# Twenty-five background steps of the next batch move from the experts' tile loop into the first feed-forward

## What is computed

```python
# block 0
h = layernorm(x) * (1 + ca) + sa
x = x + ga * attn_topk(h)        # 16 heads of 16; of each row of scores only the 32 largest count
h = layernorm(x) * (1 + cb) + sb
probs = softmax(h @ Wg + bg); e = argmax(probs) % 8
x = x + gb * relu(h @ We[e] + be[e]) * max(probs)      # "first feed-forward", 8 experts
# block 1
h = layernorm(x) * (1 + ca) + sa
x = x + ga * attn_wide(h)        # 16 heads of 64, softmax over all causal scores
h = layernorm(x) * (1 + cb) + sb
h = h + attn_small(layernorm(h) * w)                   # 16 heads of 16
y = h + moe(layernorm(h) * w2)   # router, the best 2 of 8 experts, gelu, hidden width 512
x = x + gb * y
```

## Time and profile before

| | us |
|---|---|
| three timed executions | 5928.27, 5930.14, 5935.34 |
| their median | 5930.14 |
| the profiled execution, as timed | 5932.03 |
| the profiled execution, span of its instructions | 5930.3 |

### The profile page before, as it was taken

One profiled execution on the slowest core, in us unless ns is written; L12 is line 12 of the kernel. 1 busy time (PEld: TensorE's weight loads), 2 busy tenths in 40 slices (PEclk: granted clock), 3 DMA queues, 4 the chain that ended last, 5 costly groups with the idle time before them and its releaser, 6 DMA issues. The chain is left out here.

```text
span 5930.3 us, 83316 instructions
## 1 busy us (share of the span) xinstructions
PE 4491.5 (76%) x30341; PEld 2890.1 (49%) x30341; DVE 4104.7 (69%) x8455; ACT 2753.8 (46%) x6035; POOL 1908.1 (32%) x1563
## 2 busy tenths in 40 slices
PE   4444478988677678988777688998777686999776
PEld 2333345666434454666533454666533453666334
DVE  6999957887787656888688656887778655222630
ACT  2444424666244533666345351666445360554333
POOL 2565512444323421444323430444333431000001
PEclk7656689999788889999888788999888797999888
DMA  3000000000301120000121121000031201000312
GB/s 124 11 12 25 1 22 25 18 13 15 57 12 63 48 96 22 15 16 18 36 33 35 69 76 48 13 13 13 15 54 32 75 30 50 16 10 10 63 63 72
DMA packets 113333, 213.59 MB, mean 36 GB/s; under 512 B 25728, under 2 KB 70632, under 8 KB 109552
## 3 DMA queue, kind: packets, MB, share of 16 engines
q1 hardware_dynamic: 104736, 190.94, 11.8%
q0 software_dynamic: 6144, 16.79, 0.9%
q10 hardware_dynamic: 2048, 0.53, 0.0%
HBM read 154.38 MB, written 49.73 MB: 34 GB/s over the span
## 5 line engine op out<-in xcount | busy, mean ns | idle before, releaser
L1492 DVE MAX8 vals<-work 128x8 f32<-128x128 f32 (+7 forms) x1536 | 1080.7, 743 | 0.4
L1866 POOL TENSOR_SCALAR keep<-ssb,vals 128x128 bf16<-128x128 f32 (+7 forms) x512 | 876.4, 1723 | 0.0
L469 PE MATMUL ring<-ident,pr 128*128 128x128 f32 x2304 | 490.9, 334 | 423.8 <-POOL pr L1871 372.2
L1506 DVE MATCH_REPLACE8 work<-vals,work 128x128 f32<-128x128 f32 (+7 forms) x1024 | 750.6, 739 | 0.0
L1853 POOL TENSOR_TENSOR pool_step<-ones 128x2 f32<-128x2 f32 x256 | 50.0, 195 | 2132.1 <-DVE vals L1492 2131.6
L576 PE MATMUL pA<-SC 128*128 128x512 f32 (+3 forms) x1536 | 615.6, 510 | 82.8 <-DVE SC L1635 42.3
L1871 POOL TENSOR_TENSOR pr<-keep,pr 128x128 f32<-128x128 bf16 (+7 forms) x512 | 649.0, 1289 | 0.0
L469 PEld LDWEIGHTS ring<-ident,pr 128*128 128x128 f32 x2304 | 334.8, 171 | 573.4 <-POOL pr L1871 395.5
L1143 ACT ACTIVATE prT<-ring 128x512 f32<-128x512 f32 (+1 forms) x768 | 380.5, 498 | 407.2 <-PE ring L469 405.8
L1621 DVE TENSOR_REDUCE nmax<-pA 128x1 f32<-128x1024 f32 (+7 forms) x512 | 384.4, 751 | 259.6 <-PE pA L577 248.0
L1492 DVE MAX8 vals<-ssb 128x8 f32<-128x128 f32 (+7 forms) x512 | 363.0, 750 | 263.7 <-ACT ssb L1131 246.8
(11 more groups left out here) (225 smaller groups left out, 7968.9 us busy)
## 6 DMA issues: line engine op xcount, KB each, us to landing
SC<-in_w SPq DMA_DIRECT2D x64, 512.0 KB, 7.3
stage<-parts SPq DMA_DIRECT2D x384, 64.0 KB, 2.4
parts<-SC SPq DMA_DIRECT2D x72, 256.0 KB, 2.5
SC<-parts SPq DMA_DIRECT2D x144, 128.0 KB, 7.9
SC<-in_wqkv SPq DMA_DIRECT2D x32, 384.0 KB, 2.9
rows_out<-SC SPq DMA_DIRECT2D x92, 128.0 KB, 1.7
SC<-rows_in SPq DMA_DIRECT2D x20, 512.0 KB, 3.9
SC<-in_ffn_we SPq DMA_DIRECT2D x4, 2048.0 KB, 10.3
```

The source lines that it names most:

```text
L469: mm = pe.transpose(r[:, blk % 4 * P:blk % 4 * P + P], pr0[:, p % 2, blk * P:blk * P + P], ident[:, :])
L1492: m = v.max(vals0[:, y, i, 8 * n:8 * n + 8], src[:, lo:hi])
L1506: done[i] = cht.mark(v.match_replace(out=work0[:, lo:hi], in_to_replace=vals0[:, y, i, 8 * n:8 * n + 8], in_values=src[:, lo:hi], imm_valu ...
L1866: pool.tensor_scalar(keep0[:, lo:hi], ssb0[:, p % 2, lo:hi], vals0[:, p % 2, i, TOPK - 1:TOPK], None, ALU.is_ge).then_inc(s["k"], 1)
```

## The change

The background gets a new place, called "ffn", with 8 points and a share of 0.05 of the 493 ticks, ahead of all others. The share of the experts' loop falls from 0.19 to 0.14. The other shares keep their size, so each stage between the two carries the same number of ticks as before, but from a tick 24.65 further on. Each engine gets calls `at("ffn", t)` in the first feed-forward: PE after the bias product of tile t, DVE after the update of X of tile t, ACT and SP in a row after their own work there, and POOL between the two halves of the norm that follows, which is cut in two for it. The due ticks at the eight points are 3, 6, 9, 12, 15, 18, 22, 25.

```diff
--- before.py
+++ after.py
@@ -138,8 +138,8 @@
 class Pace:
 
 
-    STAGES = (("wide", 8 * 17, 0.51), ("prep", 12, 0.04), ("flip", 8 + 48, 0.22), ("route", 6, 0.04),
-              ("moe", 23, 0.19))
+    STAGES = (("ffn", 8, 0.05), ("wide", 8 * 17, 0.51), ("prep", 12, 0.04), ("flip", 8 + 48, 0.22), ("route", 6, 0.04),
+              ("moe", 23, 0.14))
 
     def __init__(self):
         self.at, done = {}, 0.0
@@ -524,7 +524,7 @@
                     if end:
                         at("prep", t)
 
-            def ffn(b):
+            def ffn(b, at):
                 emptied(("n1", b, 3))
                 for t in range(NT):
                     if t >= 2:
@@ -561,6 +561,7 @@
                         pe.wait_ge(f0["x"], b * NT + t)
                     pe.matmul(pV[:, 0:D], gT[:, t * P:t * P + P], be[:, :], start=True, stop=True)\
                       .then_inc(f0["yb"], 1)
+                    at("ffn", t)
 
             def wide(b, at):
                 s = a1
@@ -838,7 +839,7 @@
                 pe.wait_ge(t0["nm"], b * 8 + 8)
                 project(b, [oall0[:, g, :] for g in range(4)], 4, wo0, t0, False, at)
                 norm("n1", b)
-                ffn(b)
+                ffn(b, at)
                 norm("n2", b)
                 wide(b, at)
                 project(b, oall_w, 8, wo1, a1, True, at)
@@ -1041,6 +1042,8 @@
                 sp.dma_start(we, ffn_we).then_inc(f0["w"], 16)
                 if b + 1 < B:
                     narrow_parts(0, b + 1, lambda name, i: None)
+                for t in range(NT):
+                    at("ffn", t)
                 sp.wait_ge(f0["x"], b * NT + NT)
                 sp.dma_start(wo1, wo[1]).then_inc(a1["wo"], 16)
                 wide(b, at)
@@ -1839,12 +1845,14 @@
             c.mark(pool.memset(vall0[:, :, 0:16 * VC].rearrange("p t (h d) -> p t h d", d=VC)[:, :, :, 16], 1.0))
             assert c.n == N_CONST
 
+            def half_norm(n, b, h):
+                pool.wait_ge(ln[n]["var"], b * 2 + h + 1)
+                pool.tensor_tensor(rstd[:, 4 * h:4 * h + 4], ve[:, 4 * h:4 * h + 4], mhalf[:, 0:4], ALU.pow)\
+                    .then_inc(ln[n]["rs"], 1)
+
             def norm(n, b):
-
                 for h in range(2):
-                    pool.wait_ge(ln[n]["var"], b * 2 + h + 1)
-                    pool.tensor_tensor(rstd[:, 4 * h:4 * h + 4], ve[:, 4 * h:4 * h + 4], mhalf[:, 0:4], ALU.pow)\
-                        .then_inc(ln[n]["rs"], 1)
+                    half_norm(n, b, h)
 
             carried, chosen, normal = [0], [0], [0]
 
@@ -1956,7 +1964,10 @@
                 pool.wait_ge(pj[0]["dr"], min(b + 2, B) * 192)
                 pool.wait_ge(s_x, b * 16 + 16)
                 pool.memset(qm, 0.0).then_inc(s_qz, 1)
-                norm("n2", b)
+                for h in range(2):
+                    for t in range(4 * h, 4 * h + 4):
+                        at("ffn", t)
+                    half_norm("n2", b, h)
                 wide(b, at)
                 for t in range(NT):
                     at("prep", t)
```

## The result

The changed kernel takes 5956.1 us (median of 6 runs, 5955.1 to 5958.4) against 5930.6 us (5928.3 to 5938.5) of the kernel before on the same chip: a ratio of 1.0040, 95% interval 1.0029 to 1.0052. It is slower by 0.4%, where the forecast was 5922 us. The two profiled executions have spans of 5930.3 and 5955.5 us.

A forecast was written before the change was run, and what follows sets the result against it. No engine bounds the whole span; PE paces the first feed-forward, DVE is busiest in the small attention. Batch 0 +1.0, batches 1 and 2 -4.5 each, together -8.0 us: 5924.0 from 5932.0, 5922 against the median; range 5888 to 5952.

The forecast's parts named there:

- The first feed-forward: First feed-forward: 25.6 us of DVE ticks, 8.9 hidden in its idle, the rest lengthens the stage: +16.8 us a batch.
- POOL's cover: First feed-forward: POOL's two selections fit between the half norms at no cost; if not, up to 6 us a batch.
- The wide attention: Wide attention: same 251 ticks without the empty first ones, groups starting at other phases: 577.6 against 565.7, +11.9 us.
- its classes: Wide attention: group lengths fall in two classes by first tick's phase, mean 71.5 us at r = 3, 65.1 at r = 0.
- The rival of the classes: Wide attention: the two classes are not real; 58 us in all at full price, half gives 5951; chance 0.14.
- The preparation: Preparation: the second reciprocal and spread leave it for the wide attention's group 7; -5 us, upper end 7.0.
- The small attention: Small attention: keeps 109 full ticks and its spread; 0, with -5 to +5 us for the phase.
- The routing: Routing: selections come between the scatter DMAs, the last scatter starts 6.3 us later, the following wait shortens; +3 us, at most +6.3.
- The experts' loop: Experts' loop: fewer ticks and less PE idle, 125 us; -25.7 us in batch 0, -31.2 in batches 1 and 2.
- The lower clock's 5 us: Experts' loop, batches 1 and 2: 5 us of longer PE busy time at a lower clock, counted as gained.
- The rival of a longer selection loop: Experts' loop: a selection step spans one tile more, 4.15 us; 12 us a batch, 36 in all, 5958; chance 0.14.
- PE's clock in the feed-forward: First feed-forward rival: new waits halve PE's clock, 4 us in each of five tiles, 60 us in all, 5982; chance 0.05.

The follow-up runs named there:

- the 14-tick kernel: Changed kernel with later spreads, but 14 ticks in the first feed-forward, taken from the wide attention, experts' loop share as before: 5910.2 us, ratio 0.9961.
- the one spread out of POOL's way: Changed kernel with only the small attention's spread moved, from k = 378 to k = 381: 5939.0 us, ratio 1.0020 to the kernel before.
- later spreads: Changed kernel with the three inner spreads three ticks later, the last two later: 5920.9 us; the same three inner moves in the kernel before: 5922.3 us.
- the half norm ahead of the selection: The 14-tick kernel, but POOL gives the norm's second half before its last feed-forward point: 5900.4 us, ratio 0.9956 to the kernel before.
- 13 ticks: Later spreads, ticks 0 to 12 in the first feed-forward, taken from the wide attention; tick 13 with POOL's selection stays there: 5929.7 us, ratio 0.9999.

## Why the prediction was wrong, step by step

**The first feed-forward was right.** +17.1 to +18.3 measured, +16.8 forecast. DVE no longer waits for PE from tile 3 on and runs its ticks in full; a tile of three ticks takes 9.9 to 10.4 us on DVE. POOL's cover held there as written, since both selections lie clear of the half norms; the 14-tick kernel shows what it costs when it does not, 3.6 us a batch, within the 6 that the text named. Up to the last update of X the stage grew by 12.9 us for the 12.5 forecast.

**The wide attention was 2 to 4 us short**, and its classes were half right. The changed kernel's groups, first to last (three of eight rows):

```profile
944.70:1016.00 71.30, 63.29 (x461) 41.96 (x462) 51.62 (x101) 44.22 (x104) 24.34 (x20) 0.96 0.03 8
...
1155.90:1223.10 67.20, 61.29 (x492) 43.04 (x490) 55.68 (x105) 45.37 (x106) 27.24 (x23) 0.97 0.03 8
...
1365.70:1441.80 76.10, 65.20 (x503) 45.52 (x502) 59.65 (x116) 47.98 (x111) 32.55 (x28) 0.94 0.10 28
```

Group 0 is 71.3 where 71.5 was forecast, group 3 67.2 for 65.1, group 6 76.1 for 71.5, and group 4 with its spread 72.7 for 78.5. The classes of the earlier trace rows do not carry over to other phases to better than 6 us a group; the sum came out well since the errors went both ways (-5.8 in group 4, +4.6 in group 6), which is luck. The rival of the classes was the right doubt, at 8 us in all of the 58 of its full price.

**The preparation** won 8 to 9 us for 5, more than the 7.0 named as its bound. The spread and the reciprocal left it, as the text said; why they are worth more than 7.0 there was not tried.

**The small attention was the step that failed.** The text said "The small attention keeps 109 ticks and its spread, all of them full before and after: 0". The count was right and the conclusion wrong. The spread moved from the last slots of the stage into its third head group, and what one pays for it is set by what stands ahead of it on POOL (6.1 us of selection) and behind it on ACT (the stage's exponentials). The term was 0 and measured +6.8, +8.9 and +10.6 us. With the one spread out of POOL's way, 17 of the 25 us are gone and the stage is within 1 to 3 us of before; what the rest comes from stays open. The bound of 5 us a batch, taken for "the phase", came from no row. One was at hand: a selection and the scatter behind it lie 6.3 us apart, and a whole selection ahead of POOL's multiplication would have given that as the upper end for the spread in this stage; with the multiplication's 1.27 us, which the rows did not show, it is 7.6, near the 7.96 measured. I had priced that very chain in the wide attention, at 7.0 for a reciprocal and a spread, as if it were a fixed cost.

**The routing was right**: +2.5 to +3.6 for +3, by the selection that came between the scatters. From the first scatter to the last it is 31.4 us for 25.4, 6.0 more where 6.3 was forecast, and the loop starts 8.0 us after the last one, as forecast.

**The experts' loop was right in mechanism and a little too hopeful**: 127 to 129 us for 125, 2 to 4 over. PE is busy 119.4 us of 127.4 in batch 0, where 118.9 was the sum, and idle 8.0, where I took 6. The lower clock's 5 us of batch 1 and 2 were gained, as counted. The rival of a longer selection loop, the one on the slow side with a place of its own, did not happen.

**PE's clock in the feed-forward**: the mean fell from 0.91 to 0.85, and one tile's matmuls of batch 0 took 9.95 us instead of 7.13. The changed kernel's clock by stretches, from the windows view:

```profile
865.30:906.30 41.00, 37.85 (x96) 15.85 (x94) 34.11 (x83) 5.17 (x10) 3.93 (x4) 1.00 0.00 1
906.30:913.10 6.80, 5.70 (x7) 2.52 (x8) 6.52 (x17) 0.43 (x1) 3.17 (x3) 0.50 0.00 1
913.10:930.20 17.10, 14.50 (x44) 6.27 (x42) 16.59 (x39) 3.93 (x8) 4.96 (x5) 1.00 0.00 0
930.20:944.70 14.50, 3.94 (x16) 3.14 (x16) 13.00 (x34) 3.12 (x5) 2.15 (x2) 0.50 0.19 72
```

So the clock was at its lower level for 6.8 us, from within a wait of PE of 2.62 us (one tile before, it had waited 1.60), and again for the last 14.5 us, in which PE waits 10.9 us for the norm; before, that last stretch is 7.6 us long, with a wait of 4.4. The rival had one such tile right where it feared five. The Trainium skill, "TensorE: Matmul & The Clock Gate", section "HAM oscillation — how this bites in real kernels", describes a loop in which a wait brings TensorE back to its low clock in every turn. This trace agrees only in part: PE waited in two of the last five tiles and not in all, for less time than in the page's loop, and one tile ran slow. It cost nothing that the trace shows: DVE had no idle for line 546 from tile 3 on, since its tile takes longer still. The tile in PE's timeline of the changed kernel:

```profile
907.40 9.95 PE L546 MATMUL pA<-SC,hT 128*128 128x512 f32 x16 [2.62 <-DVE SC L1597]
917.28 0.69 PE L562 MATMUL pV<-be,SC 8*128 8x256 f32 x2
```

## What to carry to other kernels

When background work is shifted along a schedule, list not only how much of it each stage carries, but each rare event in it with a wait of its own, and for each, before and after, what stands ahead of it on the engine it waits for and what stands behind the waiting instruction. A short step that others wait for belongs ahead of a long one on an in-order engine, or a few ticks behind it: here moving four such steps was worth 35 us in the changed kernel and 8 us in the kernel before, where they happened to lie better. Moving 25 ticks made no difference that could be told once they were out of the way. Count the idle that is there before filling it, and then look at what the moved ticks do elsewhere: with the same later spreads and from the same place, the experts' loop, 14 ticks gave a kernel 0.28% faster than before and 25 gave 0.1%. The fastest, at 0.44%, had 14 ticks from the wide attention and the half norm ahead of the selection; of that, 0.12% is what the later spreads give by themselves. But 13 ticks, which fit the idle of the feed-forward best, gave nothing in the total.

## What the runs showed that I had not expected

The price of a background tick in the wide attention is nowhere near its average. All 251 cost 0.63 us each over the stage without background; 25 more cost 1.3 us each; taking 14 of the lightest away (7 with work on DVE, two sets of scores on PE) won 11 to 13 us, and taking 13 away instead won nothing. One tick moves the stage by 12 to 14 us, half of it as PE's busy time, at a slightly lower mean clock (0.97 for 0.99). Why that phase is good was not settled.
